# A macaron block on one core: ten feed-forward segments become eight, with a new calendar of transfers

## What is computed

```python
x = x + 0.5 * ffn(layernorm(x))      # mixture of experts, every token goes to 2 of 12
x = x + attention(layernorm(x))      # 16 heads of 8, 256 tokens, a prior added to the scores
x = x + 0.5 * ffn(layernorm(x))      # the same experts again
# ffn: logits = x @ gate.T + bias; top 2, softmax of the two;
#      experts 0..7: w2[e] @ silu(w1[e] @ x), 128 -> 256 -> 128;  experts 8..11: x itself
```

## Time and profile before

| what | value |
|---|---|
| median of 3 runs | 1086.92 us (1086.45 to 1087.32) |
| the profiled execution | 1088.94 us |
| its span, first to last instruction | 1087.0 us |
| PE busy | 907.3 us (83%) |
| DVE busy | 906.8 us (83%) |
| ACT busy | 706.7 us (65%) |
| POOL busy | 610.4 us (56%) |

### The profile page before, as it was taken

How to read it: one execution, slowest core, us unless ns; L and a number is a source line. 1 busy time by engine, 2 the same in 40 slices (tenths; PEclk the granted TensorE clock), 3 DMA queues, 4 the chain that set the end, 5 groups by cost and what they waited for, 6 DMA issues and landing times.

```text
span 1087.0 us, 37172 instructions
## 1 busy us (share of the span) xinstructions
PE 907.3 (83%) x13792; PEld 627.9 (58%) x13792; DVE 906.8 (83%) x2396; ACT 706.7 (65%) x1370; POOL 610.4 (56%) x672
## 2 busy tenths in 40 slices
PE   3376868898899989899999898999898999886882
PEld 3265743457655568455855585555585555673771
DVE  6878857898899997898499988999988999865676
ACT  2262546668876677867865778666678666776781
POOL 6571564554355445654765465565375555557775
PEclk9886986999999999999999999999999999999896
DMA  8511439326422246224822373222474126463744
GB/s 271 170 41 34 103 115 283 84 78 119 129 70 60 64 92 172 80 68 91 218 71 68 87 175 93 62 68 61 79 165 117 59 67 133 84 165 97 161 109 112
DMA packets 205390, 118.88 MB, mean 109 GB/s; under 512 B 107264, under 2 KB 195938, under 8 KB 204960
## 3 DMA queue, kind: packets, MB, share of 16 engines
q1 hardware_dynamic: 189856, 89.40, 32.3%
q0 software_dynamic: 15360, 27.10, 9.6%
HBM read 35.33 MB, written 62.42 MB: 90 GB/s over the span
## 4 chain that ended last, share of the span: by engine, by line
DVE 38%; PE 36%; issue 12%; ACT 7%; SPq 3%; DMA 2%; POOL 1%; DVEq 0%; ACTq 0%; POOLq 0%
DVE row_max L1607 12%; DVE h_lo L1498 5%; PE banks L717 5%; PE banks L746 4%; PE banks L692 3%; PE banks L509 3%; PE banks L602 3%; PE banks L604 2%; PE banks L563 2%; PE banks L605 2%; PE banks L565 2%; PE banks L564 2%; DVE stats L1287 2%; ACT probs L1010 2%; PE banks L497 2%
## 5 line engine op out<-in xcount | busy, mean ns | idle before, releaser
L1010 ACT ACTIVATE probs<-banks 128x512 f32<-128x512 f32 x512 | 278.2, 597 | 157.9 <-PE banks L717 157.8
L1089 POOL DMA_INDIRECT xg<-xs,slots x240 | 247.6, 1032 | 192.9 <-PE banks L717 86.0
L1607 DVE TENSOR_REDUCE row_max<-banks 128x2 f32<-128x512 f32 x512 | 333.8, 684 | 21.7 <-PE banks L717 19.8
L1103 POOL DMA_INDIRECT big<-yg,slots x240 | 242.5, 1010 | 139.7 <-PE banks L717 49.8
L1498 DVE TENSOR_TENSOR h_lo<-h_f,h_hi 128x512 bf16<-128x512 f32 x208 | 141.1, 687 | 70.1 <-ACT h_hi L924 66.0
L602 PE MATMUL banks<-w_all,h_hi 128*128 (+1 forms) x832 | 157.7, 223 | 46.5 <-DVE h_lo L1498 43.9
L746 PE MATMUL banks<-probs,v_op 128*32 128x256 f32 x2048 | 181.3, 385 | 5.5 <-ACT ot_sb L1003 3.1
L922 ACT ACTIVATE h_f<-banks 128x512 f32<-128x512 f32 x208 | 125.2, 602 | 80.8 <-PE banks L565 76.8
L717 PE MATMUL banks<-band_parts,thirds 96*32 96x296 bf16 (+2 forms) x4096 | 174.4, 278 | 0.0
L604 PE MATMUL banks<-w_all,h_hi 128*128 (+1 forms) x832 | 154.4, 223 | 0.0
L605 PE MATMUL banks<-w_all,h_lo 128*128 (+1 forms) x832 | 153.8, 222 | 0.0
(11 more groups left out here) (188 smaller groups left out, 1689.8 us busy)
## 6 DMA issues: line engine op xcount, KB each, us to landing
yg<-y_rows SPq DMA_DIRECT2D x84, 256.0 KB
q_in<-kq_kept SPq DMA_DIRECT2D x96, 64.0 KB
k_op<-kq_kept SPq DMA_DIRECT2D x96, 64.0 KB
xg<-zeros SPq DMA_DIRECT2D x2, 2944.0 KB, 10.5
xg<-zeros SPq DMA_DIRECT2D x2, 2432.0 KB, 14.8
kq_kept<-kq_hi SPq DMA_DIRECT2D x32, 128.0 KB
kq_kept<-kq_lo SPq DMA_DIRECT2D x32, 128.0 KB
xg<-xs,slots POOLq DMA_INDIRECT x240
```

The lines of the kernel that those rows point to most:

```text
L1010: act.activation(probs[:, q % 2, u % 4, :], banks[:, ST[u % 2], :], ACT.Exp).then_inc(A["exp_done"], 1)
L1089: pool.indirect_dma_start(xg[q], bass.IndirectOffsetOnAxis(slots[:, q % 4, c, t:t + 1], 0), xs[:, NTH[q] % 2, t, :], None, bounds_check=CA ...
L1103: pool.indirect_dma_start(y_back[:, i, c, :], None, yg[q], bass.IndirectOffsetOnAxis(slots[:, q % 4, c, t:t + 1], 0)).then_inc(gathered[i] ...
L1607: dve.tensor_reduce(row_max[:, gp, :, qt, j], banks[:, MX[(16 * b + v) % 3], :].rearrange("p (k c) -> p k c", k=2), AX.X, ALU.max).then_in ...
```

## The change

There are eight segments: 12 tiles, dense 4, 24, 24 in the first layer, then 28, 20, 10, dense 6. Blocks stand in front of turns 4, 16, 25 and 30 instead of 4, 10, 14, 18, 25 and 31. Routed groups: 19, 31, 31, 35, 27, 17 (160 in all, 176 before); dense groups 16 and 24 (32 before). Block 0 routes nothing any more; `route(2)`, which stands alone in front of it, routes 24 tiles instead of 16. The plan of a block is now a formula in the number of four-tile chunks `nk`. The combines go two to a turn, the zero-expert scalings go to new turns, and POOL's calendar is written anew. To hold the longer segments, `xn` and `y_back` become rings of 16 tiles (`XB`, `YB`), three scratch tiles share the memory of others, and the ranks move from PSUM bank 4 to bank 6. The buffers of the scatters become four of 19, 31, 31 and 35 groups; the fourth is cleared during turn 6. The core of the diff:

```diff
-    SEG = ((4, 12), (0, 4), (16, 16), (32, 16), (48, 16), (0, 16), (16, 16), (32, 16), (48, 12), (60, 4))
-    DENSE = (1, 9)
+    SEG = ((4, 12), (0, 4), (16, 24), (40, 24), (0, 28), (28, 20), (48, 10), (58, 6))
+    DENSE = (1, 7)
-    HALF = 5
+    HALF = 4
+    XB, YB = 16, 16
-    CAP = {q: groups[q] for q in ROUTED}
+    CAP = {q: groups[2] if q in (5, 6) else groups[q] for q in ROUTED}
-    PHASES = {4: (2, 4), 10: (3, 5), 14: (4, None), 18: (5, 6), 25: (6, 7), 31: (7, 8)}
-    ZERO = {-1: 2, 0: 3, 4: 4, 10: 5, 18: 6, 25: 7, 31: 8}
+    PHASES = {4: (2, 3), 16: (3, 4), 25: (4, 5), 30: (5, 6)}
+    ZERO = {-1: (2, 0, 24), 4: (3, 0, 12), 5: (3, 12, 24), 16: (4, 0, 14), 17: (4, 14, 28), 25: (5, 0, 10),
+            26: (5, 10, 20), 30: (6, 0, 10)}
...
-    for j in range(8):
+    for j in range(12):
         added(5 + j, 0, 2, 2 * j, 2 * j + 2)
-    for b, t0, t1 in ((13, 0, 2), (14, 2, 6), (15, 6, 10), (16, 10, 14), (17, 14, 16)):
-        added(b, 0, 3, t0, t1)
-    for b, t0, t1 in ((18, 0, 4), (19, 4, 6), (20, 6, 8), (21, 8, 10), (22, 10, 12), (23, 12, 14), (24, 14, 16)):
+    for j in range(9):
+        added(17 + j, 0, 3, 2 * j, 2 * j + 2)
+    added(25, 2, 3, 18, 20)
+    added(26, 0, 3, 20, 24)
+    for b, t0, t1 in ((27, 0, 4), (28, 4, 6), (29, 6, 8), (30, 8, 12), (31, 12, 16)):
         added(b, 0, 4, t0, t1)
-    for b, t0, t1 in ((24, 0, 2), (25, 2, 6), (26, 6, 10), (27, 10, 14), (28, 14, 16)):
-        added(b, 2 if b == 24 else 0, 5, t0, t1)
-    added(30, 0, 6, 0, 4)
-    added(31, 0, 6, 4, 8)
-    added(31, 4, 6, 8, 16, 2)
+    added(31, 4, 4, 16, 24, 2)
+    added(32, 0, 4, 24, 28)
...
-            at = {"stats": (0, 1, 2, 3), "moments": (1, 3), "rows": (3, 5, 7, 9), "split": (4, 6, 8, 10),
-                  "turn": (6, 8, 10, 12), "gate": (7, 9, 11, 13), "first": (14, 15), "second": (16, 17),
-                  "ranks": (19,), "weigh": (19,), "weights": (19,), "bases": (20,), "slots": (21, 22)}
+        at = {"stats": range(nk), "moments": [min(2 * h + 1, nk - 1) for h in range((nk + 1) // 2)],
+              "rows": [3 + 2 * k for k in range(nk)], "split": [4 + 2 * k for k in range(nk)],
+              "turn": [6 + 2 * k for k in range(nk)], "gate": [7 + 2 * k for k in range(nk)],
+              "first": (2 * nk + 6, 2 * nk + 7), "second": (2 * nk + 8, 2 * nk + 9),
+              "ranks": (2 * nk + 11,), "weigh": (2 * nk + 11,), "weights": (2 * nk + 11,), "bases": (2 * nk + 12,),
+              "slots": (2 * nk + 13, 2 * nk + 14)}
         if nxt in DENSE:
-            at = {"stats": (0,), "moments": (0,), "rows": (1,), "turn": (3,), "gate": (4,), "low": (5,),
-                  "first": (5,), "second": (6,), "weigh": (7,), "weights": (8,), "mix": (9,)}
+            at = {"stats": (0, 0), "moments": (0,), "rows": (1, 2), "turn": (3, 4), "gate": (4, 5), "low": (5, 6),
+                  "first": (6,), "second": (7,), "weigh": (8,), "weights": (9,), "mix": (10,)}
...
                 if b == -1:
+                    load_x(3)
                     clear(*ROOM[3])
-                    load_x(4)
-                    clear(*ROOM[8])
-                if b == 28:
-                    store_out(5)
+                if b == 6:
+                    clear(*ROOM[4])
...
-                wait(pool, combined, TB[q] + t1 - TS)
+                wait(pool, combined, TB[q] + t1 - YB)
...
-            beside_block(scatter_rows, 2, 0, 12, 0, root=3)
+            beside_block(scatter_rows, 2, 0, 8, 0, over=(1, 11))
             batch_norm(1)
+            beside_block(scatter_rows, 2, 8, 14, 0, over=(12, 7))
             gather_rows(0, 0, 2)
             batch_norm(2)
             gather_rows(0, 2, 4)
...
+            for b in range(4, 15):
+                t1 = t0 + (3 if b in (6, 10) else 2)
                 spread(gather_rows, 2, 2 * b - 8, 2 * b - 6, b, 4)
+                spread(scatter_rows, 3, t0, t1, b, 4, 4)
+                t0 = t1
...
+            for b in range(16, 24):
+                t1 = t0 + 4 - b % 2
+                spread(gather_rows, 3, 2 * b - 32, 2 * b - 30, b, 4)
+                spread(scatter_rows, 4, t0, t1, b, 4, 4)
+                t0 = t1
...
+            for b, t0, t1 in ((25, 0, 5), (26, 5, 9), (27, 9, 13), (28, 13, 17)):
+                spread(gather_rows, 4, 2 * b - 50, 2 * b - 48, b, 4)
+                spread(scatter_rows, 5, t0, t1, b, 4, 4)
+            spread(scatter_rows, 5, 17, 20, 29, 4)
+            spread(gather_rows, 4, 8, 10, 29, 4, 4)
+            beside_block(gather_rows, 4, 10, 24, 5, root=6, over=(1, 18))
+            beside_block(scatter_rows, 6, 0, 2, 5, over=(20, 6))
+            spread(scatter_rows, 6, 2, 10, 30, 8)
+            spread(gather_rows, 4, 24, 28, 31, 4)
+            spread(gather_rows, 5, 0, 4, 31, 4, 4)
+            for t in range(4, 9):
+                gather_rows(5, t, t + 1)
+            token_roots(7)
+            for t in range(9, tiles[5]):
+                gather_rows(5, t, t + 1)
+            for t in range(tiles[6]):
+                gather_rows(6, t, t + 1)
-            beside_block(gather_rows, 6, 8, 16, 7, root=8, over=(1, 14))
-            beside_block(scatter_rows, 8, 0, 4, 7, over=(15, 8))
-            spread(scatter_rows, 8, 4, 12, 31, 8)
-            gather_rows(7, 0, 4)
-            token_roots(9)
-            gather_rows(7, 4, 16)
-            for t in range(SEG[8][1]):
-                gather_rows(8, t, t + 1)
...
+                after = {p: ((5, 12 + 2 * p), (5, 13 + 2 * p)) for p in range(4)}
+                after.update((p, ((6, p - 4),)) for p in range(4, 12))
...
-                    if q == 8 and 4 <= g < 20 and g % 2 == 0:
-                        combine(7, (g - 4) // 2)
+                    if q == 6 and g in between:
+                        combine(5, between.index(g))
...
-            all_rows(2)
-            all_splits(2)
+            for k in range(chunks[2]):
+                token_norm(2, k)
             choices(2)
-            experts(0, 3)
+            experts(0)
...
-            experts(8, 9)
-            dense_experts(9)
-            for t in range(SEG[8][1]):
-                combine(8, t)
+            experts(6, 7)
+            dense_experts(7)
+            for t in range(8, tiles[6]):
+                combine(6, t)
```

More of the change, by code:

```diff
@@ L104, in build @@
     _, DE = counted(DENSE, [n // 2 for n in tiles])
+    LB, _ = counted(DENSE, chunks)
     K0 = through(chunks)
@@ L331, in build @@
         y_out = [sem(f"y_out{i}") for i in range(RY // 2)]
-        gathered = [sem(f"gathered{t}") for t in range(TS)]
+        gathered = [sem(f"gathered{t}") for t in range(YB)]
         kq_in = [sem(f"kq_in{i}") for i in range(2)]
@@ L592, in down @@
                 wait(pe, C["lo_ready"], n + 1)
[L593 removed]
+                m = g + (EB[q] if q not in DENSE else EE[6] if q == 7 else 0)
                 if g % 2 == 0:
@@ L991, in high_part, with turn @@
                                ACT.Copy).then_inc(A["kq_hi_ready"], 1)
-            def turn(b, par, ahead=True, main=True, behind=True, zero=0):
+            def turn(b, par, ahead=True, main=True, behind=True, zero=None):
                 for s in range(8):
@@ L1006, in turn @@
                         if main:
[L1007 removed]
+                            four = u // 4
                             wait(act, A["st_done"], 16 * b + u + 1)
[L1009 to L1010 removed]
+                            wait(act, A["pv_done"], 8 * b + 2 * four - 2)
+                            act.activation(probs[:, four % 2, u % 4, :], banks[:, ST[u % 2], :],
                                            ACT.Exp).then_inc(A["exp_done"], 1)
                     if zero:
[L1013 to L1014 removed]
+                        q, t0, t1 = zero
+                        for t in range(t0 + s * (t1 - t0) // 8, t0 + (s + 1) * (t1 - t0) // 8):
+                            add_zero_expert(q, t)
                     if s == 2 and b + 2 < NBATCH:
@@ L1027, in _ @@
             route(2)
-            experts(0, 3)
+            experts(0)
             turn(-1, 1, main=False, behind=False, zero=ZERO[-1])
-            turn(0, 0, behind=False, zero=ZERO[0])
+            turn(0, 0, behind=False)
             for b in range(1, NBATCH):
@@ L1033, in _ @@
                     experts(*PHASES[b])
-                turn(b, b % 2, ahead=b < NBATCH - 1, zero=ZERO.get(b, 0))
+                turn(b, b % 2, ahead=b < NBATCH - 1, zero=ZERO.get(b))
             turn(NBATCH, 0, ahead=False, main=False)
-            experts(8, 9, [(9, t) for t in range(tiles[9])])
-            dense_experts(9)
+            experts(6, 7, [(7, t) for t in range(tiles[7])])
+            dense_experts(7)
         @block.gpsimd
@@ L1202, in _ @@
             gather_rows(0, 2, 4)
-            spread(gather_rows, 0, 4, 8, 0, 8)
-            spread(gather_rows, 0, 8, 12, 1, 8)
-            spread(scatter_rows, 2, 12, 16, 2, 8)
-            spread(scatter_rows, 3, 0, 4, 3, 8)
-            beside_block(scatter_rows, 3, 4, 9, 2, root=4)
-            for b in range(4, 7):
```

(24 more changed lines are left out.)

139 lines of the change are left out of this document (62 added, 77 removed).

## The result

| | forecast | measured |
|---|---|---|
| time, us | 1068 (1050 to 1085), from 1086.92 | 1082.68 (1080.3 to 1086.5), from 1089.37 measured beside it |
| ratio to before | 0.983 | 0.9942, 95% interval 0.9931 to 0.9953 |
| profiled execution | span -18.8 us | 1082.87 us, span 1081.1, so -5.9 |

A forecast was written before the change was run, and what follows sets the result against it. Plain blocks bound by PE, routing blocks by PE and DVE alternately, block 0 by DVE. Blocks -22.7, start -7, turns -4, late load +1.5 and end +13.4 sum to -18.8 from span 1087.0: 1068 us, range 1050 to 1085.

The forecast's parts named there:

- r: Routing's added time in the four blocks between turns: 15, 18, 12.5 and 6.5 us, together 52, near linear in tiles.
- rival C: Blocks: routing grows faster than its tiles; half way to the square, 62 us, gives 1078, full square 1088; chance 0.2.
- C's own sign: A block routing 28 tiles that takes over 70 us would show routing growing faster than its tiles.
- The load wait: Block after turn 29: SP's loads wait for segment 5's last scatters, which stand in turn 29; +1.5 us.
- 0, or up to 5 if that cover is gone: Turn 6's clear holds SP perhaps 15 us; loads queued behind are wanted mid turn 8: 0, or up to 5 us.
- Rival D: Turns 16 to 28: POOL becomes the bound; at 1.6 us a transfer, 35 us in all, 1103; chance 0.07.
- The start: Up to turn 0: -7 us, from 10.3 later start of block 0, then -14, -1.5 and -2; bounds +2 and -14.
- it costs nothing: Turn 0's gathers: POOL's 28 scatters ahead end some 2 us before turn 0 begins, so 0 us, little in hand.
- The end: Last routed block onward: POOL's root 7.4 us later, DVE waiting some 13, then +6; +13.4 us, bounds 0 and +22.
- the term of -8: End: only three us of combines after the last sum instead of eleven, since segment 6's gathers end beside dense groups: -8.
- Rival B: End: POOL finds its root early, so the 13 us DVE stall falls away, giving 1055; chance 0.18.
- E: The start gains nothing and the end costs 22 us: 1084, small gains remain; chance 0.1.

The follow-up runs named there:

- the doubled runs: Changed kernel with the rank matmuls of every routing issued twice: 1090.99 us; with the first three wide DVE operations of the choice done twice: 1087.13 us.
- statistics apart: Changed kernel with statistics of chunks 4, 5 and 6 moved from groups 4, 5, 6 to 6, 8, 10, moments with them: 1079.45 us.
- the kernel with five edits: Changed kernel with root earlier, two clears and load_x(3) in the prologue, segment 5 scattered earlier, later chunks' statistics set apart: 1051.63 us.

## Why the prediction was wrong, step by step

- **The blocks, the step that failed: r.** "I take r = 15, 18, 12.5, 6.5 ... The value lies near the linear one, since the steps of a chunk are most of the work." The blocks with 24, 28 and 20 tiles came out 1.8, 3.2 and 1.3 us above the forecast, and with 10 tiles r was 8.0 instead of 6.5; which fixed part that last one is wasn't taken apart. Together r is 60, not 52. Against the routing of 16 tiles before, scaled by the tiles, with 1.35 us for every group and read up to the next turn, the three blocks are 1.8, 3.7 and 1.8 too long: 0.3, 0.9 and 0.4 in the chunk steps; 0.7, 1.0 and 0.3 in the choice, of which 6.75 us are free however many tiles there are; 0.5, 0.9 and 0.2 in the ranks, by their columns at the pace of 2.3 us for 5208; 0.3, 0.9 and 0.8 in what stands behind the ranks. So the chunk steps were near the linear value, and what follows them was not. Choice and ranks are shown by the doubled runs to be paid in full, and of the chunk steps the run with statistics apart takes back 2.7 us. The part behind the ranks is read from the trace alone. With 28 tiles the slots come so late that the last two `h_lo` stand behind them, and from the last hidden value (ACT) to the next turn it is 6.4 us, where it is 4.1 and 4.2 with 24 and 20 tiles; ACT in order, then DVE in order:

```profile
577.06 0.59 ACT L921 ACTIVATE h_hi<-banks 128x512 bf16<-128x512 f32 x1
```

```profile
578.28 0.17 DVE L1403 TENSOR_SCALAR slots<-slot 128x28 int32<-128x28 f32 x1
578.37 1.29 DVE L1497 TENSOR_TENSOR h_lo<-h_f,h_hi 128x512 bf16<-128x512 f32 x2
```

  The sum of 60 is nearly rival C's half way to the square (62), by the cause that it named: both engines near full, so that what is late isn't made up. C's own sign, over 70 us for the block with 28 tiles, didn't come; it took 66.8.
- **The base.** Blocks before were put at 257.1 together; read from turn to turn they were 259.3, since the last two, after turns 24 and 30, are 0.7 and 1.4 longer than the 44.5 that was put for each. That error made the forecast gain 2 too small.
- **The load wait**, +1.5 forecast, was 4.8 in entry time (7.2 us from the last exponential to the first hidden value, instead of 2.4). I had looked at where the scatters stand in the calendar, not at how late POOL would be there: it issues turn 28's eight back to back into turn 29. The run with the earlier scatter shows it.
- **The turns.** "0, or up to 5 if that cover is gone": it was gone, +3.9 in turn 8, shown by the moved clear. The other turns between the blocks are 16.7 to 18.3 us, shorter where there are fewer combines, as forecast. Rival D, POOL as the bound, is false: POOL's transfers take 1.00 us in the mean (page of after), and no turn from 16 to 28 ends on POOL. The rule that I weighed, the Trainium skill's "SBUF — State Buffer", section "SBUF: two separate sides", gives 3.1 us for a transfer beside a DVE copy, and it speaks of DVE in a two-port mode. No run here shows such a time, with DVE 82% busy over the span; the prediction held the rule against all of DVE's work, but which of DVE's instructions run in that mode isn't shown, so this does not refute it.
- **The start.** Block 0's first hidden value came 10.8 us later (forecast 10.3), and it lasted 33.6 (33). The step that failed is "it costs nothing" for turn 0's gathers: I compared issue times only. They were issued as turn 0 began, but the first tile's were there only 8 us later, among a load and a clear that fill the DMA engines. Without these turn 0 is 6.8 us shorter, and the start gains 10.2 (12.3 in the kernel with five edits), nearer the better end of its bounds.
- **The end** was right in its mechanism, a wait of 11.6 us for the root. That its size fits as well, +13.5 for +13.4, is luck: two terms were off and cancel. From turn 31's last exponential to DVE's first `rows` of the last segment it is 10.9 us more than before, not 7.4, mostly since POOL's list took 101 us from the block's first gather to there instead of 98. And from there to the end it is 76.9 after 74.3, so +2.6, not +6, since behind the last sum of the dense groups (DVE in order, to be read against the earlier trace rows) 7.6 us are left of 19.2; the term of -8 should have been -11.6.

```profile
1073.46 1.25 DVE L1461 SCALAR_TENSOR_TENSOR x_all<-banks,mix,x_all 128x128 f32<-128x128 f32 x4
```

  What the forecast didn't see is that the price belongs to the root's place and not to the new segments: the root needs no gather, and eight transfers further up it is nearly free. Rival B, no wait, is false for the kernel as changed and true for the one with the early root.
- **The rest.** E, no gain at the start and 22 at the end, has the right time (1084) for the wrong stages: start and end were near the forecast, and what was missing was missing in the blocks.

## What to carry to other kernels

A step that hides in the slack of a pace-setting loop has a free allowance per iteration, not a price per element: read the slack (plain pace less the engine's own work) and charge only what exceeds it, so larger batches cost more than in proportion unless they get more iterations as well. When a queue's list grows, look in it for the short step that another engine awaits and ask what it really depends on; its place, not the list's length, cost 12 us here. A transfer's cover must be judged by its landing with the traffic of that stretch, not by its issue.
